# Expert blocks of 256 rows of one expert with stationary first weights, in a two-layer mixture-of-experts and spectral attention kernel

## The reference

```python
def _L0_ffn_ref(x, ...):
    shared_out = silu(xf @ sw1) * (xf @ sw3) @ sw2
    s = sigmoid(xf @ router_w.T)
    _, topk_idx = top_k(s + router_bias, 2)        # 8 experts
    h = gelu(einsum('nd,edh->neh', xf, ew1))       # 256 -> 256
    y = einsum('neh,ehd->ned', h, ew2)
    routed_out = einsum('ned,ne->nd', y, comb)     # comb: two gates, else 0
    return shared_out + routed_out
x = x + 0.5 * ffn(layernorm(x))
x = x + attn(layernorm(x))     # rfft, unit magnitudes, cumsum of k*v, irfft
x = x + 0.5 * ffn(layernorm(x))
```

## Time and profile before

| | |
|---|---|
| runs | 1908.44, 1908.54, 1914.2 us; median 1908.54 |
| profiled execution | 1914.37 us, span 1912.5 us |
| busy in the span | PE 1524.1 us (80%), DVE 1297.0 (68%), POOL 850.9 (44%), ACT 740.8 (39%) |
| mean granted clock of TensorE | 0.923 |
| stage B | about 421 to 702 us and 1556 to 1835 us |

### The profile page before, as it was taken

How to read it: one execution, slowest core, us unless ns; L and a number is a source line. 1 busy time by engine, 2 the same in 40 slices (tenths; PEclk the granted TensorE clock), 3 DMA queues, 4 the chain that set the end, 5 groups by cost and what they waited for, 6 DMA issues and landing times. The chain is left out here.

```text
span 1912.5 us, 35484 instructions
## 1 busy us (share of the span) xinstructions
PE 1524.1 (80%) x10030; PEld 1354.9 (71%) x10031; DVE 1297.0 (68%) x3148; ACT 740.8 (39%) x1161; POOL 850.9 (44%) x948
## 2 busy tenths in 40 slices
PE   2899999939999965777777874999999849999930
PEld 1777777739999965677777763777777749999930
DVE  4777888734555536899999855778887635555557
ACT  4333343314444423555555533343333224444410
POOL 1444444404444432666666642544545314444420
PEclk9999999969999986899999986999999979999975
DMA  8211111124444432111111001111111134444469
GB/s 286 88 52 51 55 47 45 57 63 127 133 134 134 128 125 66 45 44 44 44 44 44 0 1 48 55 46 45 52 50 54 49 85 133 133 134 133 131 212 348
DMA packets 123780, 170.36 MB, mean 89 GB/s; under 512 B 14880, under 2 KB 105392, under 8 KB 123440
## 3 DMA queue, kind: packets, MB, share of 16 engines
q1 hardware_dynamic: 89936, 91.05, 16.2%
q0 software_dynamic: 25344, 70.29, 10.1%
q10 hardware_dynamic: 8448, 8.39, 1.3%
HBM read 91.03 MB, written 81.89 MB: 90 GB/s over the span
## 5 line engine op out<-in xcount | busy, mean ns | idle before, releaser
L412 POOL DMA_INDIRECT results<-b_yb,b_goal x272 | 261.5, 961 | 368.0 <-DVE b_yb L1134 296.3
L401 POOL DMA_INDIRECT lists<-a_rows,a_slots x256 | 265.3, 1036 | 117.5 <-issue 64.5
L1134 DVE COPY b_yb<-bank 128x512 f32<-128x512 f32 x136 | 94.1, 692 | 195.8 <-PE bank L649 183.5
L647 PE MATMUL bank<-a_sw2h,a_uh 128*128 128x256 f32 x512 | 152.2, 297 | 37.5 <-DVE a_xtl L908 30.5
L476 ACT ACTIVATE a_uh<-a_gate_u 128x512 fp32r<-128x512 f32 x128 | 77.1, 624 | 255.0 <-PE bank L649 202.1
L476 ACT ACTIVATE b_hth<-bank 128x512 fp32r<-128x512 f32 x136 | 81.5, 599 | 242.9 <-PE bank L773 239.7
L647 PE MATMUL bank<-ew_h,b_hth 128*128 x544 | 162.8, 299 | 15.9 <-DVE b_htl L908 7.7
L647 PE MATMUL bank<-t_wfh,t_xah 128*128 128x256 f32 x384 | 126.2, 329 | 57.9 <-DVE t_xal L908 57.9
L647 PE MATMUL bank<-ew_h,b_xbth 128*128 x544 | 166.3, 306 | 0.6 <-DVE b_xbtl L908 0.4
L648 PE MATMUL bank<-ew_l,b_xbth 128*128 x544 | 154.8, 284 | 0.0
L649 PE MATMUL bank<-ew_h,b_xbtl 128*128 x544 | 154.6, 284 | 0.0
(11 more groups left out here) (190 smaller groups left out, 4776.9 us busy)
## 6 DMA issues: line engine op xcount, KB each, us to landing
b_xb<-lists SPq DMA_DIRECT2D x272, 132.0 KB
t_yg<-results SPq DMA_DIRECT2D x32, 512.0 KB, 4.7
f_yf<-results SPq DMA_DIRECT2D x32, 512.0 KB, 10.8
X<-in_L_attn_x SPq DMA_DIRECT2D x16, 512.0 KB, 4.1
out<-X ACTq DMA_DIRECT2D x16, 512.0 KB, 7.2
results<-b_yb,b_goal POOLq DMA_INDIRECT x272
w_raw_ew<-in_L_ffn_ew SPq DMA_DIRECT2D x2, 2048.0 KB, 12.6
lists<-a_rows,a_slots POOLq DMA_INDIRECT x256
```

The costliest lines, as they stand in the source:

```text
L401: pool.indirect_dma_start(out=lists, out_offset=bass.IndirectOffsetOnAxis(ap=slots[:, q, k, j:j + 1], axis=0), in_=rows[:, q, j, :], in_of ...
L412: pool.indirect_dma_start(out=results, out_offset=bass.IndirectOffsetOnAxis(ap=goal[:, slot, blk:blk + 1], axis=0), in_=YB[:, slot, blk, : ...
L647: pe.matmul(o, a("h"), b("h"), start=first, stop=False)
L1134: dve.tensor_copy(YB[:, slot].rearrange("p b d -> p (b d)"), bank[:, 7 - par, :]).then_inc(s_yok, 1)
```

## The change

Stage B runs over 71 blocks of 256 rows (`PAIRS`), each of one expert, instead of 68 pairs of blocks of 128. The first product is turned round: the expert's first weight is stationary and XBT (256 rows) moves, so that its result is the hidden block already transposed, and the transposes of HB are gone. For that, ACT copies the high part of the block's first weight from EW to a buffer W1 of two places, and DVE the low part; both read the expert's number from the table. Gelu writes HB, and ACT and DVE make HT's halves from HB in SBUF, in the same step. PE reads one expert number a step. DVE's goals copy, with its wait for the scatter, moves to the end of the step, and SP's loads wait for it. One transfer loads 256 rows of XB. The padding behind each list is 256 rows, the spare rows double, and the table has 71 entries of each kind. The diff, cut to its core (the table's arrays and the sizes of lists and fills follow the constants):

```diff
...
 HR = 256
-CAP = TOKENS + P
+BR = 2 * P
+CAP = TOKENS + BR
 ROW = D + 8
-BLOCKS = TOPK * TILES + E
-PAIRS = BLOCKS // 2
+PAIRS = (TOPK * TOKENS + E * (BR - 1)) // BR
+FULL = TOKENS // BR
+SPARE = E * BR
+TURNS = [(PAIRS - i + 3) // 4 for i in range(4)]
 LN_EPS, FFT_EPS, GATE_EPS = 1e-5, 1e-8, 1e-9
...
-        HB = place("b", "hb", [P, 2, 2, HR], F32)
-        HT = {h: place("b", f"ht{h}", [P, 2, KD, 2, P], F32R) for h in "hl"}
+        HB = place("b", "hb", [P, 2, 2 * HR], F32)
+        HT = {h: place("b", f"ht{h}", [P, 2, KD, BR], F32R) for h in "hl"}
+        W1 = {h: place("b", f"w1{h}", [P, 2, KD * HR], F32R) for h in "hl"}
         YB = place("b", "yb", [P, 4, 2, D], F32)
         goal = place("b", "goal", [P, 4, 2], I32)
-        over = place("b", "over", [1, E, TILES], F32)
-        past = place("b", "past", [1, 2, BLOCKS, E], F32)
-        line = place("b", "line", [1, 6, BLOCKS], F32)
+        over = place("b", "over", [1, E, FULL], F32)
+        past = place("b", "past", [1, 2, PAIRS, E], F32)
+        line = place("b", "line", [1, 6, PAIRS], F32)
 
         WF = {h: place("t", f"wf{h}", [P, KD, 3, D], F32R) for h in "hl"}
         WI = place("t", "wi", [P, 2, D], F32)
...
+                    end = sp.value_load(table[0:1, 2 * PAIRS + e:2 * PAIRS + e + 1], min_val=e * CAP,
                                         max_val=e * CAP + TOKENS)
-                    sp.dma_start(lists[bass.ds(end, P), :], fill[e * P:(e + 1) * P, :]).then_inc(s_tail, 16)
+                    sp.dma_start(lists[bass.ds(end, BR), :], fill[e * BR:(e + 1) * BR, :]).then_inc(s_tail, 16)
                 sp.wait_ge(s_tail, E * 16 * (layer + 1))
                 sp.wait_ge(s_spare, 16)
                 sp.wait_ge(s_scat, 2 * J * 16 * CH * (layer + 1))
                 p0 = PAIRS * layer
 
                 def step(n, slot, q):
-                    atleast(sp, s_bl, n + (p0 - 3) if not isinstance(n, int) or n >= 4 else 0)
-                    for blk in range(2):
-                        row = sp.value_load(table[0:1, bass.ds(n * 2 + blk, 1)], min_val=0,
-                                            max_val=E * CAP + (E - 1) * P)
-                        sp.dma_start(XB[:, slot, blk, :], lists[bass.ds(row, P), :]).then_inc(s_xb[slot], 16)
-
-                run_steps(sp, step, 0, 4, PAIRS, PAIRS, 4)
+                    atleast(sp, s_goal, n + (p0 - 3) if not isinstance(n, int) or n >= 4 else 0)
+                    row = sp.value_load(table[0:1, bass.ds(n, 1)], min_val=0, max_val=E * CAP + SPARE - BR)
+                    sp.dma_start(XB[:, slot, :, :],
+                                 lists[bass.ds(row, BR), :].rearrange("(b p) r -> p b r", p=P)).then_inc(s_xb[slot], 16)
+
+                run_steps(sp, step, 0, 4, PAIRS - 3, PAIRS, 4)
 
             def results_in(layer):
                 for i in range(4):
-                    sp.wait_ge(s_ysc[i], YW * (layer + 1))
+                    sp.wait_ge(s_ysc[i], YW[i] * (layer + 1))
 
...
                 def step(s, u, q):
                     par = u % 2
-                    if inside(s - 1, PAIRS):
-                        act.wait_ge(s_hT, s + p0)
-                        copy(HT["h"][:, 1 - par].rearrange("p k b t -> p (k b t)"),
-                             bank[:, 4 + 1 - par, :]).then_inc(s_hh, 1)
                     if inside(s + 1, PAIRS):
                         act.wait_ge(s_bps, s + (p0 + 2))
                         copy(XBT["h"][:, 1 - par].rearrange("p k b t -> p (k b t)"),
                              bank[:, 1 - par, :]).then_inc(s_bh, 1)
+                        e = act.value_load(table[0:1, bass.ds(s + (PAIRS + 1), 1)], min_val=0, max_val=E - 1)
+                        atleast(act, s_mm1, s + p0)
+                        copy(W1["h"][:, 1 - par], EW[1, "h"][:].rearrange("p (e n) -> p e n", e=E)[:, bass.ds(e, 1), :]
+                             .rearrange("p a n -> p (a n)")).then_inc(s_w1h, 1)
                     if inside(s, PAIRS):
                         act.wait_ge(s_mm1, s + (p0 + 1))
-                        act.activation(HB[:, par].rearrange("p b n -> p (b n)"), bank[:, 2 + par, :],
-                                       ACT.Gelu).then_inc(s_gelu, 1)
-
-                run_steps(act, step, -1, 4, PAIRS - 4, PAIRS + 1, 4)
+                        atleast(act, s_hl, s + (p0 - 1))
+                        act.activation(HB[:, par], bank[:, 2 + par, :], ACT.Gelu).then_inc(s_gelu, 1)
+                        act.wait_ge(s_gelu, s + (p0 + 1))
+                        atleast(act, s_yps, s + (p0 - 1))
+                        copy(HT["h"][:, par].rearrange("p m t -> p (m t)"), HB[:, par]).then_inc(s_hh, 1)
+
+                act.wait_ge(s_table, layer + 1)
+                run_steps(act, step, -1, 4, PAIRS - 3, PAIRS, 4)
 
             def attention(s, par, half):
...
+                    return pe.snap(offset[par], min_val=0, max_val=E - 1)
+
+                def expert(w, h, e, lo, n):
                     v = EW[w, h][:].rearrange("p (e n) -> p e n", e=E)
-                    return v[:, bass.ds(e, 1), k * HR:(k + 1) * HR].rearrange("p a n -> p (a n)")
+                    return v[:, bass.ds(e, 1), lo:lo + n].rearrange("p a n -> p (a n)")
 
                 def step(s, u, q):
                     par = u % 2
-                    if inside(s - 1, PAIRS):
-                        pe.wait_ge(s_gelu, s + p0)
-                        atleast(pe, s_hl, s + (p0 - 2))
-                        for k in range(KD):
-                            for blk in range(2):
-                                ins = pe.transpose(bank[:, 5 - par, (2 * k + blk) * P:(2 * k + blk + 1) * P],
-                                                   HB[:, 1 - par, blk, k * P:(k + 1) * P], ident)
-                        ins.then_inc(s_hT, 1)
                     if inside(s + 1, PAIRS):
                         slot = (u + 1) % 4
...
                         atleast(pe, s_gelu, s + (p0 - 1))
-                        for blk in range(2):
+                        for m in range(KD):
                             for k in range(KD):
-                                ins = three(bank[:, 2 + par, blk * HR:(blk + 1) * HR],
-                                            lambda h: XBT[h][:, par, k, blk, :],
-                                            lambda h: expert(1, h, at[blk], k), k == 0, k == KD - 1)
+                                ins = three(bank[:, 2 + par, m * BR:(m + 1) * BR],
+                                            lambda h: W1[h][:, par, k * HR + m * P:k * HR + (m + 1) * P],
+                                            lambda h: XBT[h][:, par, k].rearrange("p b t -> p (b t)"),
+                                            k == 0, k == KD - 1)
                         ins.then_inc(s_mm1, 1)
-                    if inside(s - 1, PAIRS):
-                        at = before
                     if inside(s + 1, PAIRS):
-                        load_experts(s + 1, 1 - par)
+                        load_expert(s + 1, 1 - par)
                     if inside(s - 1, PAIRS):
                         pe.wait_ge(s_hl, s + p0)
                         atleast(pe, s_yok, s + (p0 - 2))
                         for blk in range(2):
-                            for k in range(KD):
+                            for m in range(KD):
                                 ins = three(bank[:, 7 - par, blk * D:(blk + 1) * D],
-                                            lambda h: HT[h][:, 1 - par, k, blk, :],
-                                            lambda h: expert(2, h, at[blk], k), k == 0, k == KD - 1)
+                                            lambda h: HT[h][:, 1 - par, m, blk * P:(blk + 1) * P],
+                                            lambda h: expert(2, h, before, m * HR, HR), m == 0, m == KD - 1)
                         ins.then_inc(s_yps, 1)
 
                 pe.wait_ge(s_table, layer + 1)
-                offset = [[pe.alloc_register(f"expert_{layer}_{par}_{blk}") for blk in range(2)] for par in range(2)]
-                run_steps(pe, step, -1, 4, PAIRS - 4, PAIRS + 1, 4)
+                offset = [pe.alloc_register(f"expert_{layer}_{par}") for par in range(2)]
+                run_steps(pe, step, -1, 4, PAIRS - 3, PAIRS + 1, 4)
 
             def attention_weights():
...
             def phase_b(layer):
                 p0 = PAIRS * layer
+
+                dve.wait_ge(s_table, layer + 1)
 
                 def step(s, u, q):
                     par = u % 2
                     flat = "p k b t -> p (k b t)"
-                    if inside(s - 1, PAIRS):
-                        dve.wait_ge(s_hh, s + p0)
-                        low(HT["l"][:, 1 - par].rearrange(flat), bank[:, 5 - par, :],
-                            HT["h"][:, 1 - par].rearrange(flat)).then_inc(s_hl, 1)
                     if inside(s + 1, PAIRS):
-                        slot = (u + 1) % 4
-                        turn = q if u < 3 else q + 1
-                        atleast(dve, s_ysc[slot], turn * 32 + YW * layer)
```

(23 more changed lines are left out.)

52 lines of the change are left out of this document (24 added, 28 removed).

## The result

The changed kernel took 1922.61 us (median of 5, 1919.65 to 1926.96) against 1908.54 us (median of 5, 1907.08 to 1914.2) before: ratio 1.0075, 95% interval 1.0057 to 1.0093. It is slower by 14 us where 67 us less were forecast. The profiled execution took 1926.96 us, its span is 1925.1 us.

A forecast was written before the change was run, and what follows sets the result against it. PE was taken to set the expert stages' pace at 4.00 us a step. Two layers at -34.0 us (-68.0) and +0.7 at the start gave -67.3, from 1908.54 to 1841.2 us, range 1822 to 1884.

The forecast's parts named there:

- The forecast case, 3.38 us a step: Expert stages: 3.31 us of PE work plus 0.07 of waiting, in place of 4.00 us a step; chance 0.58.
- the 0.25 us of waiting before: Old expert step: PE waits 0.25 us for the chain from HB transposes to HT's halves; should mostly go.
- The room of 1.1 us: New expert step: gelu and HT's halves take 2.3 us while PE has 3.4 us of other work.
- 68 steps to 71: Expert stages, per layer: 68 x 4.00 = 272.0 becomes 71 x 3.38 = 240.0, -32.0 us.
- The break-even of 3.85 us a step: Expert stages: the step length, 3.38 + 67.3 / 142, above which the changed kernel would be slower than before.
- The block table: Table building: arrays of 71 instead of 136 entries, with nothing running beside it, save 2.7 us a layer.
- The weight copies: Expert step: first-weight copies add 0.62 us on ACT and 0.69 on DVE, both covered by PE's 3.38.
- Start: Kernel start: the doubled spare fill ahead of the first X costs +0.7 us, between 0 and +2.8.
- The goals copy: DVE: moved to the step's end, with two whole steps (6.8 us) for its scatter, it costs nothing.
- POOL: Rival, expert stages: DVE operations stretch scatter issues, by one or two hits a step; 3.6 us a step, 1872 us, chance 0.22.
- The hand-overs: Rival, expert stages: weight copies late for the first product make PE wait; 3.63 us a step, 1877 us, chance 0.13.
- DVE blocked by POOL: Rival, expert stages: two DVE operations each wait for a scatter issue; 4.7 us a step, 2028 us, chance 0.05.

The follow-up runs named there:

- run 5: The changed kernel unaltered, run again on another occasion: 1831.19 us, against 1877.77 us for the kernel before on its chip.
- run 12: The changed kernel unaltered, once more: 1830.39 us, against 1874.35 us for the kernel before on its chip.
- run 18: The changed kernel unaltered, on the chip of run 17: 1831.62 us, ratio 0.9753 to the kernel before.
- run 6: The kernel before, unaltered, for a trace from the same chip and hour as the experiments: 1875.44 us.
- run 8: The changed kernel with PE's signals of the XB transposes and of the first product each given half a product (0.75 us) later: 1831.97 us.
- run 15: The changed kernel with only the signal of the XB transposes given late, by nearly a whole product (1.4 us): 1914.2 us.
- run 16: The changed kernel with only the signal of the first product given late, by nearly a whole product (1.35 us): 1908.62 us.
- run 11: The changed kernel with one more transfer a step on SP's queue, a copy of 256 rows within DRAM: 1828.12 us.
- the first experiments: The changed kernel without scatters (1818.96 us), without later XB loads (1831.6), with the goals copy back (1911.75), or without the first-weight copies (1824.42).
- run 13: The changed kernel with the weight copies ahead of XBT's halves on ACT and DVE: 1884.45 us, against 1911.41 us for the kernel before.
- run 14: The changed kernel with the weight copies ahead of XBT's halves and both PE signals late by a whole product: 1908.29 us.
- run 17: The changed kernel with the weight copies ahead of XBT's halves, as in run 13: 1834.15 us, ratio 0.9764 to the kernel before.

## Why the prediction was wrong, by its steps

**The forecast case, 3.38 us a step.** PE's work of 3.31 us was exact: it is the step at the start of both layers of the recorded run and in all steady steps but one near the end of a layer (4.0 to 4.2 us) in runs 5, 12 and 18. The step that failed is the reading of the 0.25 us of waiting before, and with it the term of 0.07 us. I took it for a chain that the program makes too short and that the change loosens, and left 0.07. It was in the main lateness of PE's signals, and run 6 shows how much: with the signals on time the kernel before waits 0.06 us a step. The change doesn't remove the lateness; in the recorded run it grew, and the mean of 4.02 us is 0.71 over PE's work where 0.07 stood; at most some 0.11 of that is the half clock behind the longest pauses. Why PE's signals came late is open. The row that said so was in my hands: the high half of HT starting 1.03 us after the transposes. I used it as an argument for a rival and did not ask why a hand-over should be so slow. With the signals on time the forecast misses too: in runs 5, 12 and 18 the kernel is 44 to 47 us faster than before where 67 were forecast, and 14 of the missing 20 to 23 us come from the same misreading (below).

**The room of 1.1 us** was about right. 0.75 us of lateness are free (run 8), 1.4 are not (runs 15, 16). Beyond it the price is higher than lateness less room: 0.47 and 0.54 us where 0.25 and 0.3 were worked out. My reading, which no run separates: the room is what PE leaves; ACT and DVE work in order, and an operation that starts late there pushes the ones behind it, which belong to the other chain.

**68 steps to 71.** At an equal pace of 4.0 us this costs 3 x 4.0 x 2 = 24 us, and that is what is left once the shorter step is gone. The break-even of 3.85 us a step in the prediction gives 142 x (4.02 - 3.85) = +24, with the smaller parts as forecast. The spans differ by +12.6, since those parts came out 11 us better: a layer's first and last steps, and the time outside the expert stages, 8.2 us less in place of 3.9. Part of that is chance: before the first transpose and between the layers the recorded trace of the kernel before is 13 us longer than run 6, which has the same program, while that of the changed kernel is as long there as run 5. And in the first layer the granted clock was still 0.50 until 432.4 us in the recorded trace of before, until 425.3 in that of the changed kernel, which at about half the work is up to 3.5 us more for the former.

**The block table:** 2.9 us less a layer, forecast 2.7. **The weight copies:** 0.63 us on ACT (0.62), 0.43 to 0.45 us on DVE where I took 0.69. By the Trainium skill (VectorE: DVE Perf Modes, the perf-mode tier table) the copy runs at twice the rate of a subtraction, which I had turned into an estimate of some 0.35 us. The row lies between the two, nearer to the estimate; the copy is some 1.6 times as fast as the subtraction. **Start:** the first table entry begins 2.0 to 2.8 us later in runs 12, 18 and 5 than in run 6 (392.5 us), at the upper end of what I gave for the doubled fill, not +0.7. In the recorded pair it begins 0.3 us earlier, so it can't be seen there.

**The goals copy** "costs nothing": nearly true in its new place, 0.8 us in 160. That it would cost 80 us to leave it where it was (run 3) I did not see. It is the part of the change without which the rest is 32 us slower than before on the same chip.

**The rivals.** POOL: its scatters did stretch, from 0.959 to 1.126 us in the mean (run 5), and POOL is occupied 145.8 of 160 us there (109.2 busy, 36.6 issuing), but 3.31 us a step just hold it. Run 1, without scatters, is 12 us shorter than run 5, but only 1.6 us of that lie in the two expert stages; the rest of the kernel, which reads x in place of the results there, makes up the remainder. By the Trainium skill (SBUF — State Buffer, Who interferes with whom), which lets a DVE instruction with two SBUF inputs contend with GpSimd, the trace agrees: in run 5, between 430 and 650 us, scatter issues beside the low half of HT took 1.21 us in the median. The copy that the prediction feared beside it did not show: with the weight copy alone beside them the issues took 0.96 us in the median of 41, as in the kernel before, so the rival's second hit did not come. The hand-overs: the right rival in kind, PE idle before the second product as I wrote, but priced at 3.63 us with a chance of 0.13, while late signals give 3.8 to 4.0. DVE blocked by POOL: no, DVE's operations keep their 0.68 to 0.70 us.

**With signals on time** the sum can be checked too. From run 6 to run 5 the two expert stages lose 24.4 and 24.9 us (265.4 to 241.0, 266.2 to 241.3), where 32.0 + 0.6 - 0.9 = 31.7 were forecast against a step of 4.00; 68 x 3.81 - 71 x 3.31 is 24.1. The start takes 0.4 more, the stretch between the layers 4.6 more, the tail 0.5: -43.8 in all, the difference of the spans. The 4.6 us between the layers need not belong to the change: this stretch took 844.2 us in run 3, 844.4 in run 8, 846.3 in run 11, 848.6 in run 18 and 850.3 in run 5, all of them the changed kernel there. No run was made on it.

## What to carry to other kernels

Run the unchanged pair beside the first experiments: three edits each "cured" a stall that wasn't there on that chip. Before a wait is given to a chain in the program, measure the hand-over itself, the start of the waiting instruction less the end of the releasing one; if it varies where nothing else does, the chain needs room for it, and work that doesn't depend on the late signal belongs ahead of the wait. On an in-order engine a wait for a DMA (here 80 us, run 3) goes behind whatever the bounding engine needs.

## What the runs showed of the hardware that was not expected

PE's finish signals can come late: 2.66 us after the last matmul should be over in the case shown, while PE runs on, and the next two arrive 0.9 and 1.0 us behind it, 0.13 us apart. Both recorded kernels, run 13 and, for one signal, run 14 have it; runs 1 to 12, 17 and 18, on five chips, have them 0.30 us after the start of the matmul that gives them almost without exception. In the recorded traces a register move on SP, 0.029 us in all 94 cases of run 6 between 480 and 660 us, takes up to 0.65 us, so more than PE is touched. On the chip of runs 13 to 16 lateness was seen where PE had no pauses (run 13), in run 14 on the XB signal although PE pauses in each step, and hardly in runs 15 and 16. Doubling SP's traffic doesn't bring it about (run 11). Whether it belongs to single chips, to what else runs on them, or to the recording of the trace was not tried and stays open.
